# Attention and mixture-of-experts kernel: the second block's preparation moved into the first block's end, and GpSimd's last steps put in another order

## The reference, cut to what matters

```python
x = x + _L0_conv_ref(_ln_c(x), qkv_w, rpb, proj_w, proj_b)      # attention over 7x7 windows
t = _to_tokens(x)
t = t + _L0_ffn_ref(_ln_t(t), W_router, W1, b1, W2, b2)
...
    topk_p, topk_i = jax.lax.top_k(probs, TOP_K)                # TOP_K = 2
    topk_p = topk_p / topk_p.sum(axis=-1, keepdims=True)
    for e in range(E):                                          # E = 8
        h = jax.nn.relu(x_flat @ W1[e] + b1[e])                 # 128 -> 512
        y = h @ W2[e] + b2[e]                                   # 512 -> 128
        out = out + combine[:, e:e + 1] * y
```

## Time and profile before

| what | value |
|---|---|
| median of the runs | 3058.23 us |
| lowest and highest | 3051.5 and 3058.84 us |
| the profiled execution's own time | 3044.93 us |
| its span, first to last instruction | 3043.1 us |
| mean granted TensorE clock | 0.944 |
| PE busy | 2705.5 us (89%) |
| DVE busy | 2277.6 us (75%) |
| ACT busy | 2115.7 us (70%) |
| POOL busy | 1586.8 us (52%) |

### The profile page before, as it was taken

How to read it: one execution, slowest core, us unless ns; L and a number is a source line. 1 busy time by engine, 2 the same in 40 slices (tenths; PEclk the granted TensorE clock), 3 DMA queues, 4 the chain that set the end, 5 groups by cost and what they waited for, 6 DMA issues and landing times. The chain is left out here.

```text
span 3043.1 us, 112867 instructions
## 1 busy us (share of the span) xinstructions
PE 2705.5 (89%) x31450; PEld 2390.9 (79%) x31451; DVE 2277.6 (75%) x12559; ACT 2115.7 (70%) x5724; POOL 1586.8 (52%) x2024
## 2 busy tenths in 40 slices
PE   4799999999999999999999999999909999999733
PEld 2799998899989998999899989999806766667522
DVE  2688887788878887788778878878837878877655
ACT  1588787787878787887788868888727777777400
POOL 2145555455545554555455545555635777777600
PEclk9999999999999999999999999999959999999855
DMA  2555656565556655665555555666455444444399
GB/s 50 144 119 120 127 123 125 110 125 124 124 114 124 124 125 114 122 125 123 117 122 124 123 117 123 123 122 130 102 101 97 97 95 95 96 96 94 102 323 313
DMA packets 706127, 378.50 MB, mean 124 GB/s; under 512 B 414608, under 2 KB 662064, under 8 KB 705584
## 3 DMA queue, kind: packets, MB, share of 16 engines
q1 hardware_dynamic: 652784, 235.97, 40.1%
q10 hardware_dynamic: 24192, 81.67, 9.3%
q0 software_dynamic: 28608, 54.48, 6.0%
HBM read 233.43 MB, written 98.11 MB: 109 GB/s over the span
## 5 line engine op out<-in xcount | busy, mean ns | idle before, releaser
L980 ACT ACTIVATE pr<-sc,nmx 128x100 f32<-128x100 f32 x3136 | 924.1, 369 | 61.6 <-DVE nmx L655 60.7
L890 POOL TENSOR_TENSOR oml<-om 128x256 f16<-128x256 f32 x784 | 480.4, 613 | 893.2 <-DVE om L685 877.6
L510 PE MATMUL bank<-vwin,pt 100*128 100x65 f32 x6272 | 803.8, 271 | 29.0 <-DVE om L685 28.4
L655 DVE CUSTOM_DVE_ANT_0 sc<-bank,near 128x100 f32<-128x100 f32 x3136 | 634.1, 257 | 239.0 <-PE bank L488 199.3
L510 PEld LDWEIGHTS bank<-vwin,pt 100*128 100x128 f32 x6272 | 771.0, 194 | 46.8 <-ACT pt L988 39.8
L488 PE MATMUL bank<-kimg,qexp 128*128 (+2 forms) x9408 | 627.0, 215 | 40.2 <-issue 22.2
L488 PEld LDWEIGHTS bank<-kimg,qexp 128*128 128x128 bf16 (+1 forms) x9408 | 559.9, 100 | 87.5 <-issue 55.6
L988 ACT ACTIVATE pt<-bank 100x512 f32<-100x512 f32 x784 | 461.2, 588 | 211.4 <-PE bank L497 193.5
L1347 POOL DMA_INDIRECT yrows<-ye,meta x420 | 452.9, 1078 | 173.9 <-issue 106.7
L858 POOL DMA_INDIRECT xrows<-rows,idx x448 | 425.5, 950 | 114.4 <-issue 74.3
L497 PE MATMUL bank<-cst_sb,pr 128*100 128x128 f32 x3136 | 476.1, 275 | 0.0
(11 more groups left out here) (136 smaller groups left out, 3916.6 us busy)
## 6 DMA issues: line engine op xcount, KB each, us to landing
vwin<-v_pix SPq DMA_DIRECT2D x1120, 60.5 KB
near<-bias_rows ACTq DMA_DIRECT2D x112, 600.0 KB, 4.9
y<-yrows SPq DMA_DIRECT2D x112, 224.0 KB, 4.2
qexp<-qring SPq DMA_DIRECT2D x896, 14.0 KB
v_pix<-vrow SPq DMA_DIRECT2D x56, 225.8 KB
xin<-in_x SPq DMA_DIRECT2D x56, 224.0 KB
xres<-in_x SPq DMA_DIRECT2D x112, 112.0 KB
x<-xres SPq DMA_DIRECT2D x112, 112.0 KB
```

The costliest lines, as they stand in the source:

```text
L510: mm = pe.matmul(ps_av[m % 2][:, 2 * t + blk, :], pt[:, m % 2, 2 * t + blk, :], vwin[:, st, 2 * u + t, 64 * blk:64 * blk + 65], start=True ...
L655: i = v.tensor_tensor_reduce(out=sc[:, ring(m, par), k, :], in0=ps_s[m % 2][:, k, :], in1=near[:, st, ct, k, :], scale=-1.0, scalar=-MASKE ...
L890: g.tensor_tensor(oml[:, st, u], om[:, st, u], om_h[:, st, u], ALU.subtract).then_inc(s["oml_done"], 1)
L980: i = a.activation(pr[:, r, k, :], sc[:, r, k, :], ACT.Exp, bias=nmx[:, r, k:k + 1], scale=-1.0)
```

## The change

It does five things.

- `held`, memory that stays for both blocks, takes the place of `qexp`. Its 57,344 bytes in each partition hold the spread queries first. Once the last scores are done (`s_done`), the first half becomes `w1h`, `w1l`, `w2h`, `w2l` and the third quarter `stage2`.
- ACT's `w1h` goes between the last `t_evict` and the last `o_evict` of the first block, `w2h` to ACT's end of that block. DVE's `tables()` and `splits()` come behind its last routing step, with `near` as scratch memory. The load of `stage2` is issued by SP behind the last token load.
- The rows without effect no longer come from a tile of 15 times 4 times 520 bytes in each partition, but from two small ones: `none` (128 zeros, repeated four times by the DMA) for a row's first 512 bytes and `lost` for its last 8. Each `put_null` is now two DMAs, 30 in all.
- The seven `put_null` of the tiles behind all experts are issued in the pass J = 0, behind the load of `stage1`; the eight others at SP's end of the first block, as soon as `n_tab` is there.
- POOL's last routing steps are interleaved, and ACT's `copy_rows(PAIRS - 2)` goes behind `signs(PAIRS - 1)`.

```diff
@@ -123,6 +123,13 @@
         stage1 = sb("stage1", [128, E * FF])
         tab = sb("tab", [128, TABW])
         cap = sb("cap", [HALF, 2, E])
+        e_tab = sb("e_tab", [1, NT], I32)
+        b_tab = sb("b_tab", [1, NT], I32)
+        n_tab = sb("n_tab", [1, E], I32)
+        held = sb("held", [128, 4 * NTILE * HEADS * NQ])
+        held_b = held[:].bitcast(BF16)
+        w1h, w1l, w2h, w2l = (held_b[:, k * E * FF:(k + 1) * E * FF] for k in range(4))
+        stage2 = held[:, 2 * E * FF:3 * E * FF]
...
-        qexp = asb("qexp", [C, 2, 2, NTILE, HEADS, NQ])
-        qexp_h = qexp[:].bitcast(BF16)[:, :, :, :, :, 1::2]
-        qexp_l = qexp[:].bitcast(FP16)[:, :, :, :, :, 0::2]
+        qexp = held[:].rearrange("p (a s t h q) -> p a s t h q", a=2, s=2, t=NTILE, h=HEADS)
+        none = asb("none", [128, C])
+        lost = asb("lost", [128, 4 * (E + DUMMY), 2], I32)
+        qexp_h = qexp.bitcast(BF16)[:, :, :, :, :, 1::2]
+        qexp_l = qexp.bitcast(FP16)[:, :, :, :, :, 0::2]
...
@@ -392,6 +401,14 @@
                     if isinstance(J, int) and J == 0:
                         sp.dma_start(stage1[:].rearrange("p (e f) -> p e f", e=E), w1.rearrange("e c f -> c e f"))\
                             .then_inc(s["w1_in"], 16)
+                        sp.wait_ge(s["null_done"], 3)
+                        for k in range(DUMMY):
+                            put_null(slice(E * CAP + k * T, E * CAP + k * T + T), E + k)
+                def put_null(at_, k):
+                    to = xrows[at_, :].rearrange("(g p) w -> p g w", p=128)
+                    sp.dma_start(to[:, :, 0:C], none[:].bitcast(I32).unsqueeze(1).to_broadcast([128, 4, C])).then_inc(s["null_in"], 16)
+                    sp.dma_start(to[:, :, C:C + 2], lost[:, 4 * k:4 * k + 4]).then_inc(s["null_in"], 16)
@@ -399,6 +416,12 @@
                 for st in range(2):
                     sp.wait_ge(s[f"x1_store{st}"], 16 * PAIRS)
                 load_tokens(PAIRS - 1, (PAIRS - 1) % 2)
+                sp.wait_ge(s["s_done"], UPP * PAIRS)
+                sp.dma_start(stage2.rearrange("p (g c) -> p g c", c=C), w2.rearrange("e (f p) c -> p (e f) c", p=128))\
+                    .then_inc(s["w2_in"], 16)
+                sp.wait_ge(s["t_ready"], 1)
+                for e in range(E):
+                    put_null(bass.ds(sp.value_load(n_tab[0:1, e:e + 1], min_val=0, max_val=E * CAP), T), e)
                 sp.wait_ge(s["v_store"], V_DMAS * PAIRS)
                 for st in range(2):
                     sp.wait_ge(s[f"x1_store{st}"], 16 * PAIRS)
@@ -812,16 +835,65 @@
                         add_res(*strip_ends(PAIRS, m, PAIRS % 2, PROJECT))
                 for Q in (PAIRS - 2, PAIRS - 1):
                     for m in sorted(R_STEPS):
-                        for step in R_STEPS[m]:
-                            step(Q, Q % 2)
+                        for work in R_STEPS[m]:
+                            work(Q, Q % 2)
+
+                spare = near[0:1].rearrange("p a b c k -> p (a b c k)")
+                ind, inds = (spare[:, k * NT * E:(k + 1) * NT * E].rearrange("p (n e) -> p n e", e=E) for k in range(2))
+                rest = spare[:, 2 * NT * E:]
+                more = rest[:, 0:E * NTHR].rearrange("p (e n) -> p e n", e=E)
+                rest = rest[:, E * NTHR:]
+                cumw = rest[:, 0:(E + 1) * E].rearrange("p (a b) -> p a b", b=E)
+                rest = rest[:, (E + 1) * E:]
+                cnt, ntile, step, cum = rest[:, 0:E], rest[:, E:2 * E], rest[:, 2 * E:3 * E], rest[:, 3 * E:4 * E + 1]
+                ef, bf = rest[:, 4 * E + 1:4 * E + 1 + NT], rest[:, 4 * E + 1 + NT:4 * E + 1 + 2 * NT]
+
+                def tables():
+                    v.wait_ge(s["r_cap"], PAIRS + 1)
+                    v.tensor_copy(n_tab[:], cap[0:1, 0]).then_inc(s["t_ready"], 1)
+                    v.tensor_tensor(cnt, cap[0:1, 0], tcol("caps", E, 1), ALU.subtract)
+                    v.drain()
...
+                    v.scalar_tensor_tensor(out=b_tab[:], in0=tcol("iota", NT, 1), scalar=float(T), in1=bf,
+                                           op0=ALU.mult, op1=ALU.add).then_inc(s["t_ready"], 1)
+                def splits():
+                    v.wait_ge(s["split_h"], 1)
+                    v.tensor_tensor(w1l, stage1[:], w1h, ALU.subtract).then_inc(s["split1"], 1)
+                    v.wait_ge(s["split_h"], 2)
+                    v.tensor_tensor(w2l, stage2, w2h, ALU.subtract).then_inc(s["split2"], 1)
+                tables()
+                splits()
 
 
             @block.gpsimd
             def _(g):
                 g.memset(powc[:], -0.5)
+                g.memset(none[:], 0.0).then_inc(s["null_done"], 1)
+                g.memset(lost[:], 0).then_inc(s["null_done"], 1)
                 g.memset(ahead[:], TOK)
                 g.wait_ge(s["c_small"], 32)
                 g.tensor_copy(destf[:], tcol("dest", 2 * QT, HALF)).then_inc(s["r_first"], 1)
+                g.wait_ge(s["null_done"], 2)
+                g.tensor_copy(lost[:, :, 1:2], tcol("ndest", 4 * (E + DUMMY)).unsqueeze(2)).then_inc(s["null_done"], 1)
                 g.wait_ge(s["r_first"], 1)
                 g.memset(pad[:], 0.0).then_inc(s["pad_zero"], 1)
                 g.wait_ge(s["pad_zero"], 2)
@@ -908,12 +980,21 @@
                 pairs(g, body)
                 for m in range(L_H):
                     split_l(*back(PAIRS, m, PAIRS % 2, L_H))
-                for Q in range(PAIRS - 3, PAIRS):
-                    if Q >= PAIRS - 2:
-                        root(Q, Q % 2)
-                        split_rows(Q, Q % 2)
-                    for m in sorted(SCATTERS):
+                places_ = sorted(SCATTERS)
+
+                def scatters(Q, which):
+                    for m in places_[which]:
                         scatter(Q, Q % 2, *SCATTERS[m])
+                P2, P1 = PAIRS - 2, PAIRS - 1
+                scatters(PAIRS - 3, slice(0, 6))
+                root(P2, P2 % 2)
+                scatters(PAIRS - 3, slice(6, 8))
+                split_rows(P2, P2 % 2)
+                scatters(P2, slice(0, 4))
+                root(P1, P1 % 2)
+                scatters(P2, slice(4, 8))
+                split_rows(P1, P1 % 2)
+                scatters(P1, slice(0, 8))
 
 
             @block.scalar
@@ -1064,40 +1145,27 @@
                 for m in range(L_F + 2):
                     if m < L_T:
                         t_evict(*back(PAIRS, m, PAIRS % 2, L_T))
+                    if m == L_T:
+                        a.wait_ge(s["w1_in"], 16)
+                        a.wait_ge(s["s_done"], UPP * PAIRS)
+                        a.activation(w1h, stage1[:], ACT.Copy).then_inc(s["split_h"], 1)
                     if strip_ends(PAIRS, m, PAIRS % 2, EVICT):
                         o_evict(*strip_ends(PAIRS, m, PAIRS % 2, EVICT))
                 copy_rows(PAIRS - 3, (PAIRS - 3) % 2)
                 for Q in (PAIRS - 2, PAIRS - 1):
                     for m in sorted(R_STEPS):
                         R_STEPS[m](Q, Q % 2)
-                    copy_rows(Q, Q % 2)
+                        if Q == PAIRS - 1 and m == 7:
+                            copy_rows(Q - 1, (Q - 1) % 2)
+                copy_rows(PAIRS - 1, (PAIRS - 1) % 2)
+                a.wait_ge(s["w2_in"], 16)
+                a.activation(w2h, stage2, ACT.Copy).then_inc(s["split_h"], 1)
 
         sm.close()
 
 
-        w1h = sb("w1h", [C, E * FF], BF16)
-        w1l = sb("w1l", [C, E * FF], BF16)
-        w2h = sb("w2h", [128, E * FF], BF16)
-        w2l = sb("w2l", [128, E * FF], BF16)
-        stage2 = sb("stage2", [128, E * FF])
         b2b = sb("b2b", [128, E * C])
         b1_sb = sb("b1_sb", [128, E * FC])
-
-        null = sb("null", [128, E + DUMMY, 4, C + 2], I32)
-
...
-        b_tab = sb("b_tab", [1, NT], I32)
-        n_tab = sb("n_tab", [1, E], I32)
 
         xT = sb("xT", [C, XR, 2, T], BF16)
         meta = sb("meta", [128, MR, 4, 2])
...
@@ -1142,20 +1210,10 @@
             @block.sync
             def _(sp):
                 sp.dma_start(b1_sb[:], b1).then_inc(s["w_small"], 16)
-                sp.dma_start(stage2[:].rearrange("p (g c) -> p g c", c=C), w2.rearrange("e (f p) c -> p (e f) c", p=128))\
-                    .then_inc(s["w2_in"], 16)
                 sp.dma_start(b2b[:], bass.AP(b2.tensor, 0, [[0, 128], [1, E * C]])).then_inc(s["b2_in"], 16)
 
-                def put_null(at_, k):
-                    sp.dma_start(xrows[at_, :].rearrange("(g p) w -> p g w", p=128), null[:, k]).then_inc(s["null_in"], 16)
-                sp.wait_ge(s["null_done"], 2)
-                for k in range(DUMMY):
-                    put_null(slice(E * CAP + k * T, E * CAP + k * T + T), E + k)
-                sp.wait_ge(s["t_ready"], 1)
-                for e in range(E):
-                    put_null(bass.ds(sp.value_load(n_tab[0:1, e:e + 1], min_val=0, max_val=E * CAP), T), e)
                 sp.wait_ge(s["t_ready"], 3)
-                sp.wait_ge(s["null_in"], 16 * (E + DUMMY))
```

(36 more changed lines are left out.)

47 lines of the change are left out of this document (3 added, 44 removed).

## The result

The changed kernel took 3025.56 us (median of 4 runs, 3022.68 to 3031.42), the kernel before on the same chip 3058.53 us (4 runs, 3051.5 to 3061.77): a ratio of 0.9898, 95% interval 0.9875 to 0.9921. The profiled executions went from 3044.93 to 3022.68 us. Forecast were 3039.6 (range 3020 to 3058) and, from profile to profile, -18.6 us; measured from profile to profile were -22.3.

A forecast was written before the change was run, and what follows sets the result against it. PE's 66.8 us wait between the blocks, behind SP's chain of stores and loads, was taken as the bound. Seam -31.0 and start +12.4 gave -18.6 us: 3026.3 from the profile, 3039.6 against the median, range 3020 to 3058.

The forecast's parts named there:

- The seam: Between the two blocks: PE's wait for the experts' first transposed load shrinks by 31.0 us, between 24 and 37.4.
- POOL's order: First block's tail: interleaving covers two 2.42 us waits for ACT's rows, so the last scatter ends 4.8 us earlier.
- the hold by the splits: First block's tail: two POOL scatters wait for DVE's subtractions, 6.4 us in sum, bounds nothing and 8.8.
- DVE's tables: End of the first block, behind the last routing step: building the tables takes 6.6 us.
- The start: Pass J = 0: fourteen added DMAs hold SP up and PE loses 12.4 us.
- the scores of J = 2: First block: spread queries land at 173.2, and PE, which began here at 160.83, waits 12.4 us.
- the windows of J = 1: First block: `windows(1, 1)` comes about 5 us late, lying within the 12.4 us loss.
- SP isn't held up: Rival, pass J = 0: SP gets through in 7 us, loss only 1 us, total 3028; chance 0.16.
- the small stores are dear: Rival, J = 0 and seam: costly 8-byte stores make the kernel slower; at 130 ns, 16 us, 3074; chance 0.14.
- POOL isn't held: Rival, first block's tail: splits do not delay scatters, barrier falls 6.4 us earlier, total 3033; chance 0.10.
- The barrier: Rival, seam: POOL's drain or SP's last issues end 15 us later, halving the seam's gain; 3055; chance 0.07.
- Stretch (3): From PE's first expert product to the end; the prediction's sum had no term for it.

The follow-up runs named there:

- e5: Kernel before with only POOL's tail interleaved and ACT's `copy_rows(PAIRS - 2)` moved to match; 3053.11 us, ratio 0.9974 to the kernel before.
- e6: Changed kernel with each of DVE's two weight splits written as eight back-to-back subtractions of 512 columns; 3037.81 us, ratio 0.9922 to the kernel before.
- e11: Changed kernel with the splits in sixteen pieces of 512 columns and a drain of DVE behind each; 3027.01 us, ratio 0.9927 to the kernel before.
- e2: Changed kernel with both DVE splits moved to the start of the second block; 3024.01 us, ratio 0.989 to the kernel before.
- e9: The kernel before, unchanged, run again for a second trace; 3061.19 us, one run.
- e4: The changed kernel, unaltered, run again in a second session; 3035.70 us, ratio 0.9939 to the kernel before.
- e10: Changed kernel with splits in the second block and the seven `put_null` pairs in the first block's last two passes; 3012.95 us, ratio 0.9873.
- e1: Changed kernel with the seven `put_null` pairs at SP's end of the first block, behind the load of `stage2`, not in J = 0; 3018.01 us, ratio 0.988.
- e8: Changed kernel with the seven `put_null` pairs spread over passes 0 to 3 and both splits in the second block; 3017.19 us, ratio 0.9852.
- e7: Changed kernel with the seven `put_null` pairs spread over passes 0 to 3 in place of all in pass 0; 3024.19 us, ratio 0.9865.

## Why the prediction was right, and where it was not

**The seam: forecast -31.0, measured -29.0.** Behind the barrier all was as forecast: 39.2 us from the second block's begin to PE's first product before, 6.0 after (forecast 6.5; the issue of `b2b` 0.43 and not 0.9). POOL's order gave 4.6 of the 4.8 us (e5). The term that was mis-sized is the hold by the splits. The prediction had two scatters held for 6.4 us in sum, POOL getting in between (its bound of 8.8 was right, its middle not); the trace shows one hold of 8.6, and e6 why: POOL gets no turn between two of these subtractions that stand back to back, though each is only 0.6 us long. e11 shows the other half: with DVE empty in between for a moment, it does. What the hold cost is less than its length, some 5.6 us (e2), since without it the landing of the scatters ends the block. DVE's tables, put at 6.6 us, took 8.3 beside POOL's work (2234.38 to 2242.72).

The Trainium skill (SBUF — State Buffer, section SBUF: two separate sides) has a DVE instruction with two SBUF inputs and a GpSimd instruction that reads SBUF exclude each other for the whole instruction. The trace agrees for one instruction (e11: at most 1.48 us) and goes further: in e6 the 10.51 us went through sixteen.

**The start: forecast +12.4, measured +12.7, by another way.** Up to SP the steps came as written: SP free at 149.2 (150.7), the windows at 150.6 (151.9), the last spread query at 171.2 (171.65). But PE did not wait at the scores of J = 2. It waited for the windows of J = 1, 7.5 us where I had 5 lying within the rest, and the clock's fall to half cost nearly all of the rest, an estimated 4.6 us (half of the 9 us at 0.50), so that the spread queries were there when it came to them (0.64 us of waiting). The number is right because the queries' landing bounds both ways. I had no term for the clock: the 0.64 us are all by which the queries and not the clock still set the time, and that is luck.

**The rivals.** That SP isn't held up is out: 22.4 us for fourteen issues. That the small stores are dear is out: in the records of the single packets an 8-byte store takes 9 ns in the median (15 in the mean) and the 512-byte one 27 (49 in the mean), far below the 89 ns from which it would have decided. The Trainium skill (DMA: Bandwidth & Descriptors, section Specifications) names a read-modify-write below 512 bytes; the trace does not show that it costs anything for these. That POOL isn't held is out by 9.54 us. The barrier did take the chain's place, but only 4.2 us later than before, counted from the tail's first scatter (forecast 1.6), not 15.

**What I gave no term.** Stretch (3) became 6.6 us shorter. It is 750 to 754 us in the ten traces of kernels with the change or most of it, and 757, 763 and 767 in the three without (before, e9, e5). The first-layer products span 572 to 575 us in all of them, 2.7 of the 6.6 us; the rest lies behind the last of these, where in the gathering 50.62 MB go at 310, 300 and 300 GB/s in before, e9 and e5 and at 313 to 315 in after, e4 and e10. No instruction of the change stands there, and no run tells the cause: it stays open. Without it the profiled executions would differ by 15.5 us, the forecast being 18.6; that the 22.3 lies on the other side of 18.6 is not the prediction's merit.

**The median.** I set -18.6 against the median, 13.3 us above the profiled execution. e9 names most of those 13.3, as far as two traces can: the executions of the kernel before fall into two groups in e1's session, 3045.2 to 3049.9 with a mean granted clock of 0.944 and 3056.9 to 3061.4 with 0.940, and the two traces show the early and the late rise. In the session of the result the kernel before drew mostly late ones, by their times, and the changed one mostly early ones (0.947 in three of four), so by my estimate the 33 us of the medians hold some 10 of that draw. Like against like, early rise against early rise, it is 3044.93 to 3022.68, 22 us, and e4's 3024.34 says the same. The groups are not all of it: in e5's session the kernel before runs from 3053.9 to 3072.0 us without a gap, and in e4's the changed kernel from 3024.3 to 3043.1, more than the rise is worth. What makes the rest no trace shows.

## What to carry to other kernels

Work that is put in front of a queue's next loads costs by the first reader behind it, and a gap of 3.5 or 5.0 us on PE (e8, e2) cost 4 to 5.5 us more than its length here, for the clock that fell with it: put such stores where their queue stands idle (e10), not where it merely has room on average (e7, e8). A chain of DVE subtractions like these without a gap was one lock for POOL's scatters, with pieces of 4.4 us and of 0.6 alike; put it where POOL has nothing to send, or leave gaps, and ask first what ends the block without it: here 5.6 of 8.6 us came back. Take two profiles before setting a sum against a median: one event at the kernel's start was worth 10.4 us here, half of the effect.

## What the runs showed of the hardware that I had not expected

- The TensorE clock rose from its lower to its upper level between 100 and 110 us in seven of the thirteen traces and between 120 and 130 in the other six, behind the same PE instructions; where nothing else was moved (e5, e9, e10) the later rise put the third pass 10.0 to 10.6 us back.
- A POOL scatter of 0.94 us took 10.51 beside sixteen DVE subtractions of 0.6 us; with a drain behind each the longest took 1.48.
- The scatters' last packet ended 0.9 us after POOL's last scatter where the DMA engines were free, and 3.3 to 6.1 us after it with SP's stores beside it.
- Fourteen stores (seven of 256 KB, seven of 4 KB) behind a 2 MB load took SP 22.4 us to issue, up to 3.61 for one, while of the sixteen issues at the end of e10's first block thirteen took 0.37 each.
